# Who opens and who makes the softmax denominators' sums: VectorE, GpSimd and TensorE in a float32 attention block

## What is computed

```python
mod = (silu(c) @ wmod)                 # sa, ca, ga, sb, cb, gb for each batch element
h = layernorm(x) * (1 + ca) + sa
x = x + ga * attention(h)              # 16 heads of 32, latent k and v, a shared rotary part of 32
h = layernorm(x) * (1 + cb) + sb
x = x + gb * ffn(h)                    # r * (relu(xk @ W_k)**2 @ W_v), r = sigmoid(xr @ W_r)

# attention
scores = (q @ k.T + q_rope @ k_rope.T) / sqrt(64), causal mask
w = softmax(scores);  out = (w @ v) @ W_o
```

## Time and profile before

| | us |
|---|---|
| median of 3 runs (lowest, highest) | 3616.31 (3616.24, 3618.32) |
| the profiled execution, its own time | 3617.9 |
| its span, first to last instruction | 3616.1 |
| PE busy | 3512.0 |
| POOL busy | 2673.0 |
| DVE busy | 2561.2 |
| ACT busy | 1820.0 |
| mean granted TensorE clock | 0.99 of 2.4 GHz |

### The profile page before, as it was taken

One profiled execution on the slowest core, in us unless ns is written; L12 is line 12 of the kernel. 1 busy time (PEld: TensorE's weight loads), 2 busy tenths in 40 slices (PEclk: granted clock), 3 DMA queues, 4 the chain that ended last, 5 costly groups with the idle time before them and its releaser, 6 DMA issues. The chain is left out here.

```text
span 3616.1 us, 54216 instructions
## 1 busy us (share of the span) xinstructions
PE 3512.0 (97%) x19552; PEld 2418.5 (67%) x19552; DVE 2561.2 (71%) x5329; ACT 1820.0 (50%) x3455; POOL 2673.0 (74%) x1194
## 2 busy tenths in 40 slices
PE   8999979999999999999999999999999699999999
PEld 4777756666666666666666666666665488888887
DVE  6676777777777777777777777777775466666665
ACT  2434335555555555565555555555555344333443
POOL 2333348889898898988988989889889556666665
PEclk9999989999999999999999999999999899999999
DMA  5789763563634635546346354463561111222120
GB/s 194 267 275 301 268 168 72 114 133 84 132 86 111 138 79 117 116 93 140 83 99 149 79 122 100 94 147 77 110 145 46 62 59 69 70 70 71 70 70 35
DMA packets 232756, 426.58 MB, mean 118 GB/s; under 512 B 25380, under 2 KB 26916, under 8 KB 232488
## 3 DMA queue, kind: packets, MB, share of 16 engines
q1 hardware_dynamic: 232424, 423.10, 45.0%
q10 hardware_dynamic: 64, 0.02, 0.0%
HBM read 300.86 MB, written 121.65 MB: 117 GB/s over the span
## 5 line engine op out<-in xcount | busy, mean ns | idle before, releaser
L1022 ACT ACTIVATE att_probs<-att_ps_s 128x512 f32<-128x512 f32 (+3 forms) x2560 | 1308.4, 536 | 917.5 <-PE att_ps_s L1187 813.9
L1121 POOL TENSOR_TENSOR att_sum_g<-att_sum_g,att_probs 128x2048 f32<-128x2048 f32 (+3 forms) x400 | 1623.9, 4060 | 49.8 <-ACT att_probs L1022 1.7
L1058 DVE TENSOR_REDUCE att_piece_max<-att_ps_m 128x1 f32<-128x512 f32 x1520 | 963.2, 684 | 305.7 <-PE att_ps_m L1170 302.9
L1186 PE MATMUL att_ps_s<-att_q_a,att_k_a 128*128 128x512 f32 (+3 forms) x2560 | 952.8, 376 | 18.7 <-DMA att_q_b<-att_neg_max 9.1
L1187 PE MATMUL att_ps_s<-att_q_b,att_k_b 65*128 65x512 f32 (+3 forms) x2560 | 932.6, 368 | 0.0
L1061 DVE CUSTOM_DVE_ANT_0 att_ps_m<-att_ps_m,mask_qk 128x128 f32<-128x128 f32 x1008 | 477.5, 513 | 252.8 <-PE att_ps_m L1170 239.4
L1170 PE MATMUL att_ps_m<-att_k_a,att_q_a 128*128 128x512 f32 (+3 forms) x1808 | 644.0, 382 | 1.3 <-DVE att_piece_max L1058 0.9
L1186 PEld LDWEIGHTS att_ps_s<-att_q_a,att_k_a 128*128 128x128 f32 x2560 | 485.9, 190 | 158.8 <-issue 54.5
L1193 PE MATMUL att_ps_o<-att_probs,att_v 128*32 128x512 f32 (+3 forms) x5120 | 549.6, 536 | 10.0 <-POOL att_probs L1102 10.0
L1187 PEld LDWEIGHTS att_ps_s<-att_q_b,att_k_b 65*128 65x128 f32 x2560 | 484.8, 189 | 62.7
L1170 PEld LDWEIGHTS att_ps_m<-att_k_a,att_q_a 128*128 128x128 f32 x1808 | 337.2, 191 | 217.7 <-issue 116.1
(11 more groups left out here) (189 smaller groups left out, 4969.2 us busy)
## 6 DMA issues: line engine op xcount, KB each, us to landing
att_q_a<-s_q_hi SPq DMA_DIRECT2D x128, 256.0 KB, 6.4
att_q_a<-s_qr_hi SPq DMA_DIRECT2D x128, 256.0 KB, 7.0
prj_x_sb<-in_x_dram SPq DMA_DIRECT2D x16, 1024.0 KB, 5.3
s_q_hi<-prj_q_hi SPq DMA_DIRECT2D x16, 1024.0 KB, 4.4
s_q_lo<-prj_q_lo SPq DMA_DIRECT2D x16, 1024.0 KB, 6.5
s_k_hi<-prj_k_hi SPq DMA_DIRECT2D x16, 1024.0 KB, 4.7
s_k_lo<-prj_k_lo SPq DMA_DIRECT2D x16, 1024.0 KB, 7.1
s_v<-prj_v_sb SPq DMA_DIRECT2D x16, 1024.0 KB, 9.8
```

The lines of the kernel that those rows point to most:

```text
L1022: act.activation(probs[t % RING][:, hh, c0:CH], ps_s[(GH * t + hh) % SBANKS][:, c0:CH], ACT.Exp, scale=SCALE).then_inc(probs_ready, 1)
L1058: dve.tensor_reduce(top, ps_m[:, bank, :], AX_X, ALU.max).then_inc(piece_taken, 1)
L1121: pool.tensor_tensor(sum_g[:, :, c0:CH], sum_g[:, :, c0:CH], new, ALU.add).then_inc(sum_added, 1)
L1186: mm(out[:, c0:CH], k_a[:, hh, i * P:(i + 1) * P], q_a[j][:, hh, c0:CH], start=True, stop=False)
```

## The change

It has three parts. In `SHARE_OF` three steps of 512 columns turn from T to G (step 8 of block 2, steps 6 and 12 of block 3), and for blocks 1 to 3 the first addition, of steps 0 and 1, is made by VectorE, a head at a time, when the block before is closed; GpSimd starts with step 2. All four blocks now open `ps_d` with the closing matmuls (`OPENED_BY_SUM`). VectorE's inversions and the normalisation of blocks 0 to 2 move one step back for it, and the planner's amounts in `CLOSING` are new.

```diff
+PAD = 104
...
-SHARE_OF = ("GGTT", "GGGGGGGG", "GGGGGGGGTGGT", "GGGGGGTGGGGGTGGT")
+SHARE_OF = ("GGTT", "GGGGGGGG", "GGGGGGGGGGGT", "GGGGGGGGGGGGGGGT")
+CLEAR_AHEAD = (((0, 0), (1, 1), (2, 1), (3, 2)),
+               ((4, 4), (5, 4), (6, 5), (7, 5)),
+               ((8, 7), (9, 7), (10, 8), (11, 8)),
+               ((12, 12), (13, 13), (14, 14), (15, 14)))
...
+def pool_order(j):
+
+    order = [("add", i) for i in range(STEPS[j])]
+    for i, ahead_of in CLEAR_AHEAD[j]:
+        order.insert(order.index(("add", ahead_of)), ("clear", i))
+    return order
...
-PIECE, CLOSING = 2.8, 19
+PIECE, CLOSING = 2.8, {(0, 2): 19, **{(j, 2): 20 for j in range(1, TCH)}, **{(j, 4): 11 for j in range(1, TCH)}}
...
-    closes = lambda m: CLOSING * any(FIRST[j] + 2 == 2 * m for j in range(TCH))
+    closes = lambda m: sum(took for (j, late), took in CLOSING.items() if FIRST[j] + late == 2 * m)
...
+            def open_sum(u, j, hh):
+                if hh == 0:
+                    dve.wait_ge(closed, TCH * u + j + 1)
+                    dve.wait_ge(probs_ready, heads_ready(u, FIRST[j] + 1, GH - 1))
+                two = [probs[(FIRST[j] + i) % RING][:, hh, :] for i in (0, 1)]
+                opened = dve.tensor_tensor(sum_g[:, hh, :], two[0], two[1], ALU.add)
+                if hh == GH - 1:
+                    opened.then_inc(sum_added, 1)
+
...
             for t, (u, j) in CLOSE_AT.items():
+                if j < TCH - 1:
+                    for hh in range(GH):
+                        extras[t + 1].append(lambda u=u, j=j, hh=hh: open_sum(u, j + 1, hh))
+                later = 2 if j < TCH - 1 else 1
                 for r in range(TB):
-                    extras[t + 1 + r // 2].append(lambda u=u, j=j, r=r: invert(u, j, r))
-                extras[t + 2].append(lambda u=u, j=j: normalise(u, j))
+                    extras[t + later + r // 2].append(lambda u=u, j=j, r=r: invert(u, j, r))
+                extras[t + later + 1].append(lambda u=u, j=j: normalise(u, j))
...
                 if i == mine[1]:
-                    first = probs[(FIRST[j] + mine[0]) % RING]
+                    first = probs[FIRST[j] % RING]
                     pool.wait_ge(closed, TCH * u + j + 1)
-                    if c0:
-                        pool.tensor_copy(sum_g[:, :, 0:c0], first[:, :, 0:c0]).then_inc(sum_added, 1)
+                    pool.tensor_copy(sum_g[:, :, 0:c0], first[:, :, 0:c0]).then_inc(sum_added, 1)
...
-                    order = [(what, i) for i in range(STEPS[j]) for what in ("clear", "add")]
-                    if j == 2:
-                        for i in (TB * j - 1,):
-                            order.remove(("add", i))
-                            order.insert(order.index(("clear", TB * j + 1)) + 1, ("add", i))
-                    for what, i in order:
+                    for what, i in pool_order(j):
...
-                        if what == "add" and i in mine[1:]:
+                        if what == "add" and i in mine[1 if j == 0 else 2:]:
                             add(u, j, i, mine)
...
+            "pad": sb("pad", [P, PAD], F32),
```

More of the change, by code:

```diff
@@ L132, in projection @@
         x_sb, rot_tab, x_in, tab_in = (prj[n] for n in ("x_sb", "rot_tab", "x_in", "tab_in"))
[L133 to L136, removed]
         xn, up_raw = prj["weights"][2][0], prj["weights"][4][0]
@@ L145, in projection @@
         rot = pair("rot", [DR, 2, CH])
+        stats = sb("stats", [P, TB, 6], F32)
+        mv = sb("mv", [P, TB, 2], F32)
+        veps = sb("veps", [P, TB], F32)
+        rstd = sb("rstd", [P, TB], F32)
         ps_t = ctx.enter_context(nc.psum_tensor("prj_ps_t", [P, NC, CH], F32))
@@ L1075, in normalise @@
                 dve.tensor_tensor(o_sb[j % 2][:], o_sb[j % 2][:], ps_d[:], ALU.mult).then_inc(o_ready, 1)
-            extras = {t: [] for t in range(NU * NSTEP + LAG + 2)}
+            def open_sum(u, j, hh):
[6 more added lines that the diff above has]
+                    opened.then_inc(sum_added, 1)
+            extras = {t: [] for t in range(NU * NSTEP + LAG + 4)}
             for t, (u, j) in CLOSE_AT.items():
+                if j < TCH - 1:
+                    for hh in range(GH):
+                        extras[t + 1].append(lambda u=u, j=j, hh=hh: open_sum(u, j + 1, hh))
+                later = 2 if j < TCH - 1 else 1
                 for r in range(TB):
-                    extras[t + 1 + r // 2].append(lambda u=u, j=j, r=r: invert(u, j, r))
-                extras[t + 2].append(lambda u=u, j=j: normalise(u, j))
+                    extras[t + later + r // 2].append(lambda u=u, j=j, r=r: invert(u, j, r))
+                extras[t + later + 1].append(lambda u=u, j=j: normalise(u, j))
             for t, extra in extras.items():
@@ L1259, in feedforward @@
         w_v = pair("w_v", [P, NC, D])
-        mu = sb("mu", [P, 2, NC], F32)
         gate = sb("gate", [P, NB, 2, D], F32)
@@ L1266, in feedforward @@
         x1_kept = sb("x1_kept", [P, TB, D], F32)
[L1267 to L1271, removed]
         diff = sb("diff", [P, NC, CH], F32)
@@ L1276, in feedforward @@
         act_f = sb("act_f", [P, 2, CH], F32)
+        h2 = sb("h2", [P, NC, 1 + CH], F32)
+        mu = sb("mu", [P, 2, NC], F32)
+        stats = sb("stats", [P, TB, 6], F32)
+        mv = sb("mv", [P, TB, 2], F32)
+        veps = sb("veps", [P, TB], F32)
+        rstd = sb("rstd", [P, TB], F32)
         ps_t = ctx.enter_context(nc.psum_tensor("ffn_ps_t2", [P, NC, CH], F32))
```

## The result

The changed kernel takes 3846.13 us (median of 4 runs, 3845.88 to 3847.35). The kernel before, run beside it, takes 3617.18 (4 runs, 3616.24 to 3618.32). The ratio is 1.0634 (95% interval 1.0621 to 1.0647): 229 us slower. The forecast was 3819, the range 3646 to 3898. The profiled execution spans 3844.6 us against 3616.1, at a mean granted clock of 0.959 against 0.990.

What follows compares the result with a forecast made beforehand. POOL's add chain was taken to set S1 and S2, and after the change S3, with S0 PE's. 3617.9 + 171 (chains) + 32 (clock) = 3821 us, 3819 against the median; range 3646 to 3898.

Steps and rivals of the forecast that it cites:

- POOL's chain: Attention blocks 1 to 3: POOL's gapless adds and clears up to a closing; moved steps and opening cost 171 us.
- S1: Time from the closing of block 0 to that of block 1: forecast 31.2 us (+1.3), set by POOL.
- S2: Time from the closing of block 1 to that of block 2: forecast 46.7 us (+4.7), set by POOL.
- S3: Time from the closing of block 2 to that of block 3: forecast 66.6 us (+4.7), on POOL's chain.
- The opening: Behind closings of blocks 0 to 2: VectorE's four adds (2.5 us) free POOL of 4.6 us, gain its chain nothing.
- D: Time from the end of a closing to POOL's next add: 6.2, 4.3 and 5.0 us after blocks 0, 1, 2.
- The clock: After PE's standstills before closings the granted clock halves: 2 us a unit in S0, bounds 0 and 5; 32 us.
- S0: Time from the closing of block 3 to the next unit's block 0, PE's own: 12.15 us, plus 2 for the clock.
- Layout: Large buffers moved onto 512-byte boundaries: taken as zero for TensorE (19 us gain to 9 us cost) and for POOL.
- rival (b): S1 to S3: POOL's add gets cheaper on the boundaries, PE becomes the bound again, 3545 to 3560; chance 0.13.
- Rival (a): Behind closings: same chain but a short opening, D = 3.0 each, and the clock holds: 3700; chance 0.12.
- Rival (c): Attention: effects cancel, at an add of 4.1 to 4.2 us or as the opening adds nothing: 3616; chance 0.05.

Runs made afterwards that it cites:

- the layout run: The kernel before with only the pad and the small buffers moved, the FFN's likewise: 3607.54 us, ratio 0.9978 against the kernel before.

## Why the forecast was right, and where its steps were off

**POOL's chain.** Right, and it carries the result. The three moved steps cost 177 us by the run that took only them back, and 208 with the order of clears and the planner's amounts. S1 came out 0.15 below the forecast, S2 1.1 and S3 2.0 above. The step in block 2 alone gave 46.74, where one add more than 42.0 makes 46.7; there clear 11 still stood behind the last add. S2's 1.1 in the changed kernel are 0.5 for a closing at half clock (1.59 instead of 1.07 us on average), 0.3 for the opening and 0.3 of waiting before a clear.

**The opening.** Right. D was put at 6.2, 4.3 and 5.0 and is 6.21, 4.62 and 5.78. That an opening by VectorE frees POOL and shortens nothing holds: without it the kernel is 29 us faster. But its size was off: the forecast's steps make it 1.3 - 0.6 + 0.1 = 0.8 us a unit, 13 us; the segments show 2.0.

**What S3 lacked.** In unit 5, S3 is 68.32 long (1399.16 to 1467.48). The forecast had the add start 1.06 + 5.0 = 6.06 behind the closing's start; it came 7.71 behind it (1406.87), 1.65 later. Of that 0.87 is the closing itself, which took 1.93 at half clock instead of 1.06. The 0.78 left is the opening, whose pieces PE made in the same slow stretch; with the steps back on TensorE, where this closing ran at full clock, D was 5.05, the forecast's own value. From the first add to the closing it took 60.6 us, and the forecast's terms leave 60.5. So this unit's miss is nearly all the clock behind the standstill.

**The clock.** The 2 us a unit are about what it cost, but not where the forecast put them; that the sizes agree is luck. The forecast put 2 us a unit into S0 and named the delay of an opening, up to 1 us, only as an aside. The changed kernel's S0 runs at 1.00: PE's last standstill comes 7.6 us of work ahead of the closing of block 3, and the clock is back by then. The cost is behind the closings of blocks 1 and 2 instead, 0.5 and 0.9 us in the closings and up to 0.8 in the openings. The run with earlier clears shows that the forecast's place is real when the standstill stands there: S0 at 0.82, 15.14 us.

**PE's waits.** "Before nearly every closing of blocks 1 to 3, 5 us and more" is half right: 2.99 and 4.54 us on average before the closings of blocks 1 and 2, and none before block 3's. There the wait is for a clear, a product with V held by POOL's queue. The forecast counted a clear's 0.63 us in POOL's chain, but not who waits for it: that the probabilities are there when a clear starts was nearly true in the chains (one wait, 0.3 us on average, in block 2), but it is not the whole of a clear's place. In the changed kernel this is nearly free (0.57 us between the last add and the closing in unit 5, 0.78 on average). In the run with one step moved in block 3 it decided the sign.

**S0.** Forecast unchanged, measured +1.0. It is not the clock. The planner deals S0 14 pieces instead of 12, seven of 512 columns instead of four, and S1 27 for 29. From start to next start S0's pieces take 3.17 us instead of 2.19, which is all of it. The forecast had worked out the dealt counts around the closings, but not their sum by segment.

**Layout.** Forecast 0, within -19 and +9 for TensorE; measured -8. POOL's full add stayed (4591 to 4587 ns), so rival (b) has no ground. The Trainium skill (GPSIMD Engine Reference, "Elementwise — side-by-side cycle accounting") has 4497 ns for it; the shortest single adds come there in both layouts (4498 ns before, 4504 after), the means do not.

**Contention.** None: the 192 opening adds take 680 to 693 ns, far from the 1172 of the earlier trace rows, with POOL idle during them. By the rule that the forecast quotes from the Trainium skill (SBUF — State Buffer, "Who interferes with whom") nothing had to be held either. No run here shows the rule at work: no opening add of any run overlapped an instruction of POOL.

**The sum.** Forecast 12.7 us a unit, measured 14.5: S2 and S3 together 3.1 more, S0 1.0 less than the 2 put there. Over 16 units these 1.8 are 29 us and the layout takes 8 back, which makes 21 of the 27 us between 3819 and 3846. The first and the last unit are not like the rest (S3 is 69.84 and 66.33 long in them) and together grew 3.5 us more than two steady ones, and the kernel before ran at 3617.18 beside the changed one, 0.9 above the forecast's base. That leaves under 2 us. Rival (a) is ruled out: D is 4.6 to 6.2 instead of 3.0 and the clock did not hold; with the opening ahead of those pieces D is still 3.3 to 5.05. Rival (c) is ruled out by the result.

## What to carry to other kernels

Before work is moved from the busiest engine to another, find for each segment between two meeting points who sets its end: here the same kind of step cost 94 us in a segment of POOL's and, with its clears in order, gained 12 in one of PE's. Slack in a helper's chain is not enough; ask of every instruction in its in-order queue who waits for it, and put those ahead of the long ones. And an earlier start is worth only as much as the next operation in the chain can use, so look at what that one waits for.

## What was not expected of the hardware

The granted clock halves after short standstills within dense work. After waits of 4.04 to 4.57 us it was at 0.50 or 0.51 for the stretches of 3.5 to 4.8 us shown above, and in six of 14 units of the run with step 6 moved a wait of 1.15 us was followed by 3.4 us at 0.50. But length alone doesn't decide: with step 8 moved, waits of 3.0 to 3.4 us were followed by a closing at full speed (1.07 us) in eight units and by one at half (1.93) in four, and with the early opening and the old shares all 14 waits of 1.5 us by one at full speed. The price of one such stretch, where PE sets the end, was 1.7 us (63.9 less 62.2) to 2.1 (S0 15.14 less 13.05). Where POOL sets the end it costs only what POOL has to wait for: nothing inside S2 of the run with step 8 moved (granted clock 0.96, length 42.0 and one add), but 0.5 to 1.6 us where it covers a closing and the pieces behind it. Why 1.15 us is enough in one unit and not in the next was not settled.

FFN matmuls of 512 columns whose operands lay at different offsets from a 512-byte boundary start 233 ns apart (median, kernel before) and 227 with all on a boundary (the layout run); pairs at one offset were at 227 in both, and attention's scores stay at 233 with the boundaries. The layout gains by this outside attention; why attention's do not follow stays open, and no run moved one buffer alone.
